# Attention over sixteen-wide heads: queries and keys turned unstacked and spread by transfers, row maxima turned alone

## The chip, the cores and the metric

One core of one Trainium2 chip runs the whole program. The metric is the device time of one execution in microseconds (us); less is better. A profiled execution also has a span, from its first to its last recorded instruction.

## What is computed

The program is a chain of six blocks over x, 4 batches of 512 tokens of width 256: a mixture of experts, attention, experts again, a gated feed-forward block, an attention on sine features, and the feed-forward block again. The change lies in the softmax attention alone:

```
q, k, v = split(x @ Wqkv + bqkv)          # 16 heads of 16
q, k = rot(q), rot(k)                     # rotary: t1*c - t2*s, t1*s + t2*c
scores = q @ k.T / 4 + causal_mask
ctx = softmax(scores) @ v
x = x + ctx @ Wout + bout
```

## The kernel before

All values are 32 bits wide. A value that TensorE multiplies in its one-pass format (F32R) is split in a high half (the value rounded to the format) and a low half (the rest), and products are summed over the halves. For a head, the 16 rows of the turned query stand three times on the partitions (high, low, high) and those of the key as high, high, low, so that one matmul over 48 partitions gives all three products. A 49th row holds the negated row maximum beside the queries and 1 beside the keys: the second product of a head then comes out with the maximum already subtracted. Two heads, a pair, stand at partitions 0 and 64.

Attention goes over 32 pairs `w` (4 batches of 8 pairs), with 3 steps `t` each, 96 steps in all and some more to drain. Step t of every engine's program holds, in this order written out by hand:

- TensorE (PE): `scores(t)` (L1343), query blocks against keys, to banks 0 and 1; `shifted(t - 7)` (L1358), the transposed product with the maxima, to banks 2 and 3; every sixth step and the one after it `weigh` (L1373), probabilities times v; then a turn, a set of four 128-column transposes to bank 4 (L1313): `turn_q1(s+1)` in the first step of a pair, `turn_k(s+1)` in the second, `turn_q2(s-1)` in the third, the last one with the maxima in the stack. Behind that the next batch's work (`turn_x`, `project_qk`, `project_v`; u is the step within the batch) and the last batch's (`turn_sums`, `turn_context`, `project_half`).
- VectorE (DVE): the copy of a turned key stack (`out_k`, L1730) in the third step, rotary pieces (`rope_a` L1716, `rotate` L1723), then `maxima(t)` (L1740), which frees the score banks for the next step.
- ScalarE (ACT): the copies of the two query turns (`out_q1` L1590, `out_q2` L1596), the copies of projections, `high` (L1583, L1584), which writes the high halves of the stacks, and `exponentials` (L1606).
- GpSimd (POOL): `keep_causal` (L1245), `swapped` (L1225), a rotary piece, and `low` (L1236), which writes the low halves.
- SyncE (SP): its queue has only loads ahead of the loop and stores of finished rows late in it.

Ahead of the loop (the lead) batch 0 is projected, its rotary pieces run on DVE alone, and the first pair is turned. `spin` (L337) is matmul work with no result, to keep PE busy.

Of the kernel before, what the change touches and what calls it, by code (L numbers as in the profile page):

```python
# [14 lines left out]
P = 128  # L15
# [207 lines left out]
def program(nc, ins, out):  # L223
# [4 lines left out]
    with ExitStack() as ctx:  # L228
# [33 lines left out]
        g.route_dram = nc.dram_tensor("route_rows", (2 * TILES, P), F32, kind="Internal").ap()  # L262
        g.xn_dram = nc.dram_tensor("xn_rows", (TOKENS, D), F32, kind="Internal").ap()
# [830 lines left out]
def attention_stage(nc, g, ins):  # L1094
# [3 lines left out]
    with ExitStack() as ctx:  # L1098
# [10 lines left out]
        rot = turns("rot", [P, 2, 2 * D])  # L1109
# [10 lines left out]
        part_b = sb("part_b", [P, 2, 2 * D])  # L1120
# [3 lines left out]
        q1 = sb("q1", [P, 2, SEQ], F32R)  # L1124
        q2 = sb("q2", [P, 2, SEQ], F32R)
        kt = sb("kt", [P, 4, SEQ], F32R)
# [8 lines left out]
        a_done, b_done, rot_done, hi_done, lo_done = (  # L1135
            sem("a_done"), sem("b_done"), sem("rot_done"), sem("hi_done"), sem("lo_done"))
        q1_ps, q1_out, k_ps, k_out, q2_ps, q2_out = (
            sem("q1_ps"), sem("q1_out"), sem("k_ps"), sem("k_out"), sem("q2_ps"), sem("q2_out"))
# [20 lines left out]
        bank_of = lambda m: AFTER[m][0]  # L1159

# [6 lines left out]
        def _(sp):  # L1167
# [9 lines left out]
            for b in range(2, BATCH):  # L1177
                sp.wait_ge(g.back_here[b - 2], 32)
                load_back(sp, g, b)
            def store_x(b):  # L1180
                sp.wait_ge(x_added, 2 * b + 2)
                sp.dma_start(by_tiles(g.turned_dram[0], b), g.x[:, b * BT:(b + 1) * BT, :]).then_inc(x_stored, 16)
# [4 lines left out]
            store_x(0)  # L1187
            store_x(1)
            store_xn(0)
            store_xn(1)  # L1190
# [11 lines left out]
        def _(pool):  # L1202
            nc.gpsimd.memset(b_src[:, :], 0.0).then_inc(zeroed, 1)
            for q in range(2):
                nc.gpsimd.memset(f32(k_stack[:, q, :, :, 3 * HD:SK]), 1.0)
                nc.gpsimd.memset(f32(q_stack[:, q, :, :, 3 * HD:SK]), 0.0)
                last = nc.gpsimd.memset(v[:, q, :, :, HD:HD + 1], 1.0)
            last.then_inc(ready, 1)
            norm.rstd(pool, 0)
# [8 lines left out]
            def swapped(n):  # L1218
                pool.wait_ge(qk_out, n + 1)
                if n >= 2:  # L1220
                    pool.wait_ge(rot_done, n - 1)
                src = qk[:, n % 2, :].rearrange("p (h s e) -> p h s e", s=2, e=HALF)
                dst = part_b[:, n % 2, :].rearrange("p (h s e) -> p h s e", s=2, e=HALF)
# [6 lines left out]

            def low(n):
                pool.wait_ge(hi_done, n + 1)
                b, i = n // BT, n % BT
                halves = rot[:, n % 2, :].rearrange("p (s h d) -> p s h d", s=2, d=HD)
                for s, (stack, hi, lo) in enumerate(((q_stack, 0, 1), (k_stack, 0, 2))):
                    last = nc.gpsimd.tensor_tensor(stack[:, b % 2, i, :, lo * HD:(lo + 1) * HD], halves[:, s, :, :],  # L1236
                                                   f32(stack[:, b % 2, i, :, hi * HD:(hi + 1) * HD]), ALU.subtract)
                last.then_inc(lo_done, 1)
# [10 lines left out]
            for i in range(BT):  # L1249
                low(i)  # L1250
            biased(0)
            norm.rstd(pool, 1)
            for t in range(ALL + LAG + 1):
# [4 lines left out]
                if front < BATCH:  # L1258
# [4 lines left out]
                    elif u == 8:  # L1263
                        low(4 * front)
                    elif u == 9:
                        low(4 * front + 1)
# [4 lines left out]
                    elif u == 13:  # L1271
                        low(4 * front + 2)
                    elif u == 14:
                        low(4 * front + 3)
# [9 lines left out]
        def _(pe):  # L1284
# [24 lines left out]
            def turn_stack(w, stack, bank, done):  # L1309
                b, hp = w // PAIR, w % PAIR  # L1310
                for i in range(BT):
                    flat = f32(stack[:, b % 2, i, :, :]).rearrange("p h c -> p (h c)")
                    last = nc.tensor.transpose(g.ps[:, bank, i * P:(i + 1) * P], flat[:, hp * P:(hp + 1) * P],  # L1313
                                               g.ident[:, :])
                last.then_inc(done, 1)

            def turn_q1(w):
                pe.wait_ge(lo_done, 4 * (w // PAIR) + 4)
                if w >= 3:
                    pe.wait_ge(q2_out, w - 2)  # L1320
                turn_stack(w, q_stack, 4, q1_ps)

            def turn_k(w):
                pe.wait_ge(q1_out, w + 1)
                turn_stack(w, k_stack, 4, k_ps)

            def turn_q2(w):
                pe.wait_ge(max_done, 2 * STEPS * (w + 1))
                pe.wait_ge(k_out, min(w + 3, BATCH * PAIR))
                turn_stack(w, q_stack, 4, q2_ps)  # L1330

            def scores(t):
                w, step = t // STEPS, t % STEPS
                if step == 0:
                    pe.wait_ge(q1_out, w + 1)
                    pe.wait_ge(k_out, w + 1)
                for a in range(2):
# [3 lines left out]
                    for i in SCORES[step]:  # L1341
                        n = (i + 1) * P
                        last = nc.tensor.matmul(g.ps[:, a, col:col + n], q1[at, w % 2, i * P:n], kt[at, w % 4, 0:n],  # L1343
# [4 lines left out]
            def shifted(t):  # L1348
                w, step = t // STEPS, t % STEPS
                if step == 0:  # L1350
                    pe.wait_ge(q2_out, w + 1)
                for a in range(2):
# [3 lines left out]
                    for j in SHIFTED[step]:  # L1356
                        n = SEQ - j * P
                        last = nc.tensor.matmul(g.ps[:, 2 + a, col:col + n], kt[at, w % 4, j * P:(j + 1) * P],  # L1358
                                                q2[at, w % 2, j * P:SEQ], start=True, stop=True)
# [61 lines left out]
            for i in range(BT):  # L1421
                if i >= 2:
                    pe.wait_ge(qk_out, i - 1)
                    pe.wait_ge(v_out, i - 1)
                project_qk(0, i, 2 + i % 2)
                project_v(0, i, 5 + i % 2)
            for i in (2, 3):
                pe.wait_ge(lo_done, i)
                spin(nc, g, 0, 10)
            turn_q1(0)  # L1430
            turn_k(0)
            for t in range(ALL + LAG + 5):
# [120 lines left out]
        def _(act):  # L1553
# [6 lines left out]
            def out_qk(b, i, bank):  # L1560
                n = 4 * b + i
                act.wait_ge(qk_ps, n + 1)
                if n >= 2:
                    act.wait_ge(a_done, n - 1)
                    act.wait_ge(b_done, n - 1)
# [9 lines left out]
            def high(b, i):  # L1575
                n = 4 * b + i
                act.wait_ge(rot_done, n + 1)
                if b >= 2:
                    act.wait_ge(q2_ps, PAIR * (b - 1))
                halves = rot[:, n % 2, :].rearrange("p (s h d) -> p s h d", s=2, d=HD)  # L1580
                cols = lambda stack: stack[:, b % 2, i, :, :].rearrange("p h (c d) -> p h c d", d=HD)
                twice = lambda s: halves[:, s, :, :].unsqueeze(2).to_broadcast([P, H, 2, HD])
# [1070 lines left out]
```

## Time and profile before

| | |
|---|---|
| median of 3 runs | 1167.85 us (1167.42 to 1170.57) |
| the profiled execution's own time | 1165.93 us |
| its span | 1164.0 us |
| PE busy over the span | 1052.2 us (90%) |
| DVE, ACT, POOL busy | 731.1, 463.2, 432.6 us |
| attention's loop (about 236.6 to 506 us) | some 270 us |

### The profile page before, as it was taken

The page shows a single profiled execution, that of the slowest core. Times are in us where ns is not written, and L with a number is a line of the kernel's source. Part 1 is how long each engine was busy: PE and PEld are TensorE (multiplying, and loading weights), DVE is VectorE, ACT ScalarE, POOL GpSimd, SP SyncE. Part 2 cuts the span into 40 slices and gives each one's busy share as a digit, 9 for nine tenths or more (in the row PEclk, how much of TensorE's full clock was granted, in tenths as well). Part 3 has the DMA queues.
Part 4 walks back from the last instruction along what each step waited for, and adds up shares of the span by engine and source line. Part 5 has one row for each costly group of instructions (what it writes and reads, how often), then busy time and mean ns, then how long its engine had stood idle before and what let it go on. Part 6 is the DMA issues. An engine that isn't in the chain of part 4 may idle for free. (4 is left out here: it accounts for less than half of the span.)

```text
span 1164.0 us, 18769 instructions
## 1 busy us (share of the span) xinstructions
PE 1052.2 (90%) x6537; PEld 870.1 (75%) x6537; DVE 731.1 (63%) x1754; ACT 463.2 (40%) x806; POOL 432.6 (37%) x474
## 2 busy tenths in 40 slices
PE   4899995779999999987999987999988998899997
PEld 3778884656566665666888886888878897788886
DVE  7934443787777778557454446765648878555653
ACT  4324331327666756625243322233334434223222
POOL 3056654326362723201576521000139788300000
PEclk8699998889989998887999998999997999999999
DMA  9034422300000000117472241000010030000000
GB/s 335 31 94 144 156 80 90 108 0 2 2 1 20 1 19 19 37 37 290 143 252 91 83 162 61 1 1 1 1 73 1 4 70 1 1 1 19 19 19 19
DMA packets 36881, 72.39 MB, mean 62 GB/s; under 512 B 8180, under 2 KB 25654, under 8 KB 36536
## 3 DMA queue, kind: packets, MB, share of 16 engines
q1 hardware_dynamic: 29112, 50.21, 12.8%
q0 software_dynamic: 7680, 20.98, 5.5%
q8 instruction: 57, 0.93, 0.3%
q14 instruction: 32, 0.26, 0.1%
HBM read 47.04 MB, written 24.13 MB: 61 GB/s over the span
## 5 line engine op out<-in xcount | busy, mean ns | idle before, releaser
L2041 PE MATMUL ps<-xt,w 128*128 128x512 f32 x768 | 192.5, 401 | 7.0 <-PEq L66 7.0
L2041 PEld LDWEIGHTS ps<-xt,w 128*128 128x128 f32 x768 | 143.3, 192 | 36.9 <-issue 5.5
L1740 DVE CUSTOM_DVE_ANT_0 ps<-ps,att_mask 128x128 f32<-128x128 f32 (+3 forms) x256 | 119.1, 516 | 40.6 <-PE ps L1343 40.3
L718 PE MATMUL ps<-moe_w,moe_narrow_xb 128*128 x480 | 125.0, 395 | 0.0
L122 POOL TENSOR_TENSOR var_eps<-bn,eps 128x4 f32<-128x4 f32 x24 | 6.6, 275 | 290.5 <-DVE bn L99 265.5
L2137 DVE TENSOR_TENSOR had_gated<-ps,had_sig 128x512 f32<-128x512 f32 x64 | 44.3, 691 | 110.8 <-ACT had_sig L2094 110.8
L2094 ACT ACTIVATE had_sig<-ps 128x512 f32<-128x512 f32 x64 | 38.3, 598 | 188.7 <-PE ps L2041 188.7
L616 POOL DMA_INDIRECT moe_xs<-xn_rows,moe_index x80 | 80.7, 1009 | 75.5 <-DVE moe_index L1017 44.1
L622 POOL DMA_INDIRECT made_rows<-moe_units_made,moe_index x80 | 79.6, 994 | 74.6 <-ACT moe_units_made L845 62.1
L718 PEld LDWEIGHTS ps<-moe_w,moe_narrow_xb 128*128 128x128 f32 x480 | 90.1, 188 | 19.6
L1606 ACT ACTIVATE att_early_probs<-ps 128x384 f32<-128x384 f32 (+1 forms) x192 | 90.7, 527 | 29.4 <-PE ps L1358 28.5
L1245 POOL TENSOR_SCALAR_AFFINE_SELECT att_early_probs<-att_early_probs 128x256 f32<-128x256 f32 x128 | 53.5, 431 | 118.1 <-ACT att_early_probs L1606 118.0
L1036 DVE TENSOR_TENSOR moe_narrow_xb<-ps,moe_narrow_xb 128x512 fp32r<-128x512 f32 x40 | 27.6, 691 | 110.2 <-ACT moe_narrow_xb L827 110.1
L2055 PE MATMUL ps<-w,had_yhi 128*128 128x256 f32 x512 | 94.4, 283 | 1.8 <-DVE had_ylo L2149 1.8
L2055 PEld LDWEIGHTS ps<-w,had_yhi 128*128 128x128 f32 x512 | 82.9, 189 | 7.8 <-DVE had_ylo L2149 2.6
L827 ACT ACTIVATE moe_narrow_xb<-ps 128x512 fp32r<-128x512 f32 x40 | 23.8, 598 | 135.0 <-PE ps L702 135.0
L1343 PE MATMUL ps<-att_kt,att_q 48*128 48x256 f32 (+3 forms) x256 | 66.4, 417 | 11.8 <-DVE att_q_stack L1740 9.1
L2055 PE MATMUL ps<-w,had_ylo 128*128 128x256 f32 x256 | 72.2, 282 | 0.0
L2277 POOL TENSOR_TENSOR fea_inv_norm<-fea_norm,neg_half 128x24 f32<-128x24 f32 x16 | 66.7, 4172 | 11.3 <-DVE fea_norm L2506 11.1
L337 PE MATMUL ps<-column,ident 128*128 128x128 f32 x356 | 53.5, 320 | 18.3 <-PEq L66 11.1
L744 PE MATMUL ps<-moe_w,moe_units_yb 128*128 x480 | 67.6, 280 | 0.0
L337 PEld LDWEIGHTS ps<-column,ident 128*128 128x128 f32 x356 | 51.7, 234 | 19.8 <-issue 11.2
(276 smaller groups left out, 2320.0 us busy)
## 6 DMA issues: line engine op xcount, KB each, us to landing
moe_w<-in_moe SPq DMA_DIRECT2D x16, 768.0 KB, 8.9
back<-made_rows SPq DMA_DIRECT2D x16, 512.0 KB, 5.7
x<-x_turned SPq DMA_DIRECT2D x8, 512.0 KB, 7.9
low_weights<-moe_w SPq DMA_DIRECT2D x4, 768.0 KB, 3.6
moe_w<-low_weights SPq DMA_DIRECT2D x4, 768.0 KB, 16.7
x<-in_x SPq DMA_DIRECT2D x4, 512.0 KB, 5.5
xn_rows<-moe_wide_xn SPq DMA_DIRECT2D x4, 512.0 KB, 10.7
x_turned<-x SPq DMA_DIRECT2D x4, 512.0 KB, 2.9
```

The costliest lines, as they stand in the source:

```text
L337: nc.tensor.matmul(g.ps[:, bank, 0:P], g.ident[:, :], g.column[:, :], start=True, stop=True)
L616: nc.gpsimd.indirect_dma_start(out=xs[:, j % AHEAD, i, :], out_offset=None, in_=g.xn_dram[:, :], in_offset=at(0, 2 * j + i)).then_inc(gath ...
L622: nc.gpsimd.indirect_dma_start(out=g.made_dram[:, :], out_offset=at(1, 2 * j + i), in_=made[:, j % 2, i, :], in_offset=None) \
L718: last = nc.tensor.matmul(h_bank(j, i), xb[a][:, j % 2, i, k, :], weight(c), start=False, stop=(k == KC - 1 and c == 1))
L744: last = nc.tensor.matmul(O_BANK[:, i * D:(i + 1) * D], yb[a][:, j % 2, i, c, :], weight(q), start=False, stop=(c == IC - 1 and q == 1), s ...
L1245: last = nc.gpsimd.affine_select(block, block, [[0, 2], [1, P]], ALU.is_ge, 0.0, base=0, channel_multiplier=-1)
L1343: last = nc.tensor.matmul(g.ps[:, a, col:col + n], q1[at, w % 2, i * P:n], kt[at, w % 4, 0:n], start=True, stop=True)
L1606: nc.scalar.activation(probs[:, w % 3, a, at:at + n], g.ps[:, 2 + a, 0:n], ACT.Exp, scale=HD ** -0.5).then_inc(exp_done, 1)
L1740: last = nc.vector.tensor_tensor_reduce(g.ps[:, a, col:col + n], g.ps[:, a, col:col + n], mask[:, SEQ - n:SEQ], -1.0, 3.0e38, ALU.add, ALU ...
L2041: last = nc.tensor.matmul(g.ps[:, bank(n, half), :], w[a][:, k, c * P:(c + 1) * P], xt[low][:, b % 2, k, :], start=(k == 0 and q == 0), st ...
L2055: last = nc.tensor.matmul(o, a[:, n % 4, at], g.w2[w][:, c, :], start=(c == 0 and q == 0 and i % 2 == 0), stop=(c == HC - 1 and q == 2), s ...
L2277: nc.gpsimd.tensor_tensor(inv_norm[:, t % 4, :], norm2[:, t % 4, :], g.neg_half[:, 0:QKH], ALU.pow) \
```

## The change

Queries and keys are no longer stacked before they are turned. Four chunks per batch (queries or keys of eight heads, 128 columns; `turn_chunk`) are turned as whole values; ACT writes the high half (`high_chunk`) and DVE the low half (`low_chunk`) of the chunk behind the turn, into `stage`. SP stores both halves to DRAM (`store_chunk`, 2 transfers of 256 KB) and loads them back onto their partitions (`load_chunk`, 6 transfers of 128 KB). The first pair's rows are copied directly, 6 transfers on SP and 6 on ACT. The maxima are written to `shift`, two columns for each block of rows, turned alone (`turn_shift`, 2 rows of 512), copied by ACT (`out_shift`) and put in the 49th row by two transfers of 2 KB (`place_shift`). The turns of the maxima stand in the second step of a pair and those of chunks in the third. In the lead the rotary piece `swapped` goes from DVE to POOL, and `rope_a` now waits for it; the stores of finished rows take their turn behind the loop's transfers.

```diff
-        q_stack = sb("q_stack", [P, 2, BT, H, SK], F32R)
-        k_stack = sb("k_stack", [P, 2, BT, H, SK], F32R)
-        kt = sb("kt", [P, 4, SEQ], F32R)
+        stage = sb("stage", [P, 2, 2, SEQ], F32R)
+        shift = sb("shift", [P, 3, BT, 2], F32R)
+        shift_row = sb("shift_row", [P, SEQ], F32R)
+        qt = sb("qt", [P, 2, H // 2, SEQ], F32R)
+        kt = sb("kt", [P, 2, H // 2, SEQ], F32R)
...
+        COPIES = ((0, 1, 0), (0, 0, 1))
+        def chunk_at(s):
+            if s in (1, 2):
+                return s + 1
+            b, c = (s // PAIR, 3) if s % PAIR == 0 else (s // PAIR + 1, s % PAIR - 5)
+            return 4 * b + c if s >= 5 and c >= 0 and b < BATCH else None
...
+            def store_chunk(n):
+                sp.wait_ge(chunk_hi, n + 1)
+                sp.wait_ge(chunk_lo, n + 1)
...
+                for half in range(2):
+                    sp.dma_start(g.spread_dram[c, half], f32(stage[:, n % 2, half, :])).then_inc(stage_stored[n % 2], 16)
+            def load_chunk(n):
...
+                sp.wait_ge(stage_stored[n % 2], 32 * (n // 2 + 1))
...
+                for a, rows, half in copies(n):
+                    mine = g.spread_dram[c, half].rearrange("(m a d) n -> a d m n", a=2, d=HD)[a]
+                    sp.dma_start(f32(stacked[n % 2][rows, b % 2, 4 * (c // 2) + begin:4 * (c // 2) + 4, :]),
+                                 mine[:, begin:, :]).then_inc(rows_here[c], 16)
+            def place_shift(w):
+                sp.wait_ge(shift_out, w + 1)
+                for a in range(2):
+                    at = 64 * a + 3 * HD
+                    sp.dma_start(f32(qt[at:at + 1, b % 2, hp, :]), f32(shift_row[a:a + 1, :])).then_inc(shift_here, 16)
...
+            for s in range(1, BATCH * PAIR + 1):
+                if chunk_at(s) is not None:
+                    store_chunk(chunk_at(s))
+                place_shift(s - 1)
+                if chunk_at(s) is not None:
+                    load_chunk(chunk_at(s))
...
+            def turn_rows(n, i):
+                return nc.tensor.transpose(g.ps[:, chunk_bank(n), i * P:(i + 1) * P], rot[:, i, at:at + P], g.ident[:, :])
...
+            def turn_shift(w):
+                pe.wait_ge(max_done, 2 * STEPS * (w + 1))
...
+                for i in range(BT):
+                    last = nc.tensor.transpose(g.ps[0:2, CHUNK_BANK, i * P:(i + 1) * P], f32(shift[:, w % 3, i, :]),
                                                g.ident[:, :])
...
-                if step == 0 and s + 1 < BATCH * PAIR:
-                    turn_q1(s + 1)
-                elif step == 1 and s + 1 < BATCH * PAIR:
-                    turn_k(s + 1)
-                elif step == 2 and 1 <= s <= BATCH * PAIR:
-                    turn_q2(s - 1)
+                if step == 1 and 1 <= s <= BATCH * PAIR:
+                    turn_shift(s - 1)
+                elif step == 2 and chunk_at(s + 1) is not None:
+                    turn_chunk(chunk_at(s + 1), s)
...
-                if step == 0 and 2 <= s < BATCH * PAIR + 2:
-                    out_q2(s - 2)
-                elif step == 1 and s + 1 < BATCH * PAIR:
-                    out_q1(s + 1)
+                if step == 2 and 1 <= s <= BATCH * PAIR:
+                    out_shift(s - 1)
+                elif step == 0 and chunk_at(s) is not None:
+                    high_chunk(chunk_at(s))
...
-                if step == 2 and s + 1 < BATCH * PAIR:
-                    out_k(s + 1)
+                if step == 0 and chunk_at(s) is not None:
+                    low_chunk(chunk_at(s))
```

## Rows read from the trace of the kernel before

**Rows 1.** Windows of the lead and of each batch's 24 steps.

```profile
core 0: us, PE busy (x) PEld busy (x) DVE busy (x) ACT busy (x) POOL busy (x), PEclk, DMA share, GB/s
211.00:236.60 25.60, 19.94 (x104) 17.48 (x104) 20.99 (x39) 8.91 (x17) 11.05 (x11) 0.83 0.09 30
236.60:300.00 63.40, 57.03 (x349) 37.63 (x350) 50.28 (x178) 36.77 (x74) 25.89 (x43) 0.89 0.00 1
300.00:363.00 63.00, 60.73 (x452) 41.00 (x452) 47.77 (x162) 40.70 (x85) 29.33 (x49) 0.95 0.01 1
363.00:428.00 65.00, 63.03 (x470) 42.56 (x467) 46.61 (x160) 42.65 (x89) 28.89 (x49) 0.95 0.03 9
428.00:484.00 56.00, 53.27 (x383) 32.31 (x383) 44.28 (x171) 33.76 (x69) 15.10 (x36) 0.88 0.09 30
```

**Rows 2.** Waits in the loop, 236 to 506: us in total, times, longest.

```profile
PEld ps L1343 <- DVE att_q_stack L1740: 14.8, 47, 0.8
PEld ps L1313 <- ACT att_q L1590: 5.2, 13, 0.5
```

**Rows 3.** Timeline of PE: start, length, instructions; a turn and what follows it.

```profile
371.48 0.66 PE L1313 MATMUL ps<-ident,att_q_stack 128*128 128x128 f32 x4
371.89 0.48 PE L1294 MATMUL ps<-att_b_row,ones 128*128 128x512 f32 x1
...
432.35 0.66 PE L1313 MATMUL ps<-ident,att_q_stack 128*128 128x128 f32 x4
432.93 0.50 PE L1343 MATMUL ps<-att_kt,att_q 48*128 48x128 f32 x4
```

**Rows 4.** Timeline of DVE: the third and the first step of two pairs, back to back.

```profile
295.64 0.68 DVE L1730 CAST att_kt<-ps 128x512 fp32r<-128x512 f32 x1
296.24 0.69 DVE L1740 CUSTOM_DVE_ANT_0 ps<-ps,att_mask 128x512 f32<-128x512 f32 x1
...
297.63 0.30 DVE L1740 CUSTOM_DVE_ANT_0 ps<-ps,att_mask 128x128 f32<-128x128 f32 x1
...
298.86 0.14 DVE L1740 DVE_READ_ACCUMULATOR2_ANT att_q_stack<- 128x1 fp32r x1
```

**Rows 5.** Groups by form, attention's whole stage.

```profile
L1225 POOL TENSOR_TENSOR att_part_b<-att_qk,att_rope_s 128x256 f32<-128x256 f32 x24 | 20.5, 875 | 16.0 <-ACT att_qk L1566 16.0
L1596 ACT ACTIVATE att_q<-ps 128x512 fp32r<-128x512 f32 x32 | 19.4, 607 | 8.2 <-PE ps L1313 8.1
L1206 POOL MEMSET att_q_stack<- 128x1024 f32 x2 | 1.9, 959 | 0.0
```

**Rows 6.** DMA issues with the median time to landing, then SP's timeline of issues.

```profile
x<-x_turned SPq DMA_DIRECT2D x8, 512.0 KB, 7.9
x_turned<-x SPq DMA_DIRECT2D x4, 512.0 KB, 2.9
route<-route_rows SPq DMA_DIRECT2D x1, 16.0 KB, 1.9
...
485.21 0.36 SPq L1182 DMA_DIRECT2D x_turned<-x  x1
578.52 2.00 SPq L575 DMA_DIRECT2D x<-x_turned  x4
```

**Rows 7.** Timeline of the end of the lead, all engines.

```profile
228.07 1.16 DVE L1723 TENSOR_TENSOR att_turns_rot<-att_turns_rot,att_part_b 128x512 f32<-128x512 f32 x1
230.95 4.31 DVE L1804 SCALAR_TENSOR_TENSOR x<-back,route,x 128x256 f32<-128x256 f32 x4
236.65 0.50 PE L1343 MATMUL ps<-att_kt,att_q 48*128 48x128 f32 x4 [0.88 <-DVE att_kt L1730]
237.70 0.29 DVE L1740 CUSTOM_DVE_ANT_0 ps<-ps,att_mask 128x128 f32<-128x128 f32 x1
```

**Rows 8.** Windows of 3.3 us in the loop, columns as in the first group.

```profile
325.70:329.00 3.30, 2.45 (x16) 1.49 (x14) 3.30 (x11) 2.61 (x6) 3.30 (x6) 1.00 0.00 0
329.00:332.30 3.30, 3.30 (x17) 3.15 (x17) 2.68 (x10) 1.47 (x3) 2.93 (x5) 0.51 0.00 0
...
464.30:467.60 3.30, 2.38 (x15) 1.62 (x14) 3.27 (x12) 0.71 (x2) 0.48 (x1) 1.00 0.44 153
470.90:474.20 3.30, 3.30 (x18) 2.17 (x20) 2.17 (x6) 1.68 (x3) 0.41 (x1) 0.50 0.03 7
```

More of the change, by code:

```diff
@@ L1159, in attention_stage, with chunks_turned, chunk_bank, copies @@
         bank_of = lambda m: AFTER[m][0]
+        COPIES = ((0, 1, 0), (0, 0, 1))
+        CHUNK_BANK = 4
+        LEAD_CHUNKS = 2
+        stacked = (qt, kt)
+        def chunk_at(s):
[3 more added lines that the diff above has]
+            return 4 * b + c if s >= 5 and c >= 0 and b < BATCH else None
+        def chunks_turned(s):
+            return LEAD_CHUNKS + sum(chunk_at(q) is not None for q in range(1, s + 1))
+        def chunk_bank(n):
+            return 0 if n == 1 else CHUNK_BANK
+        def copies(n):
+            for a in range(2):
+                for c, half in enumerate(COPIES[n % 2]):
+                    yield a, slice(64 * a + HD * c, 64 * a + HD * (c + 1)), half
         def at_step(t, offset):
@@ L1186, in store_xn @@
                 sp.dma_start(by_tiles(g.xn_dram[:, :], b), g.xn[:, b % 2, :, :]).then_inc(xn_stored[b], 16)
[L1187 to L1190, printed above, removed]
+            sp.wait_ge(chunk_hi, 1)
+            sp.wait_ge(chunk_lo, 1)
+            for a, rows, half in copies(0):
+                sp.dma_start(f32(qt[rows, 0, 0, :]), f32(stage[HD * a:HD * (a + 1), 0, half, :])).then_inc(direct_here[0], 16)
+            for n in range(LEAD_CHUNKS):
+                store_chunk(n)
+            for n in range(LEAD_CHUNKS):
+                load_chunk(n)
+            BESIDE = {2 * PAIR: (store_x, 0), 3 * PAIR: (store_x, 1), 3 * PAIR + 3: (store_xn, 0), 3 * PAIR + 6: (store_xn, 1)}
+            for s in range(1, BATCH * PAIR + 1):
[4 more added lines that the diff above has]
+                    load_chunk(chunk_at(s))
+                if s in BESIDE:
+                    store, b = BESIDE[s]
+                    store(b)
             store_x(2)
@@ L1229, in swapped @@
                 last.then_inc(b_done, 1)
[L1231 to L1238, printed above, removed]
             def keep_causal(t):
@@ L1249, in _ @@
             for i in range(BT):
-                low(i)
+                swapped(i)
+            set_ones(1)
             biased(0)
@@ L1332, in scores @@
             def scores(t):
                 w, step = t // STEPS, t % STEPS
-                if step == 0:
-                    pe.wait_ge(q1_out, w + 1)
-                    pe.wait_ge(k_out, w + 1)
+                b, hp = w // PAIR, w % PAIR
+                if w == 0 and step == 0:
+                    pe.wait_ge(chunk_hi, LEAD_CHUNKS)
+                    pe.wait_ge(chunk_lo, LEAD_CHUNKS)
+                    for kind in range(2):
+                        pe.wait_ge(direct_here[kind], 96)
+                elif step == 0:
+                    for kind in range(2):
+                        pe.wait_ge(rows_here[2 * (hp // 4) + kind], 96 * (b + 1))
@@ L1632, in _ @@
             act.wait_ge(ready, 1)
-            out_qk(0, 0, 2)
-            out_v(0, 0, 5)
-            for i in range(1, BT):
+            for i in range(BT):
                 out_qk(0, i, 2 + i % 2)
+            for i in range(BT):
                 out_v(0, i, 5 + i % 2)
-                high(0, i - 1)
-            high(0, BT - 1)
-            out_q1(0)
+            for n in range(LEAD_CHUNKS):
+                high_chunk(n)
+            act.wait_ge(chunk_hi, 2)
+            act.wait_ge(chunk_lo, 2)
+            act.wait_ge(ones_set, 1)
+            for a, rows, half in copies(1):
+                nc.scalar.dma_start(f32(kt[rows, 0, 0, :]), f32(stage[HD * a:HD * (a + 1), 1, half, :])) \
+                    .then_inc(direct_here[1], 16)
             for t in range(ALL + LAG + 5):
@@ L1836, in _ @@
                 rope_a(i)
-                swapped(i)
                 rotate(i)
-                if i == 1:
-                    add_back(2, 0)
+            for n in range(LEAD_CHUNKS):
+                low_chunk(n)
+            add_back(2, 0)
             dve.wait_ge(combined, 8)
@@ L1843, in _ @@
             add_back(2, 1)
-            out_k(0)
             for t in range(ALL + LAG + 5):
```

194 lines of the change are left out of this document (84 added, 110 removed).

## The prediction

> **What bounds the kernel now.** I read the page first: TensorE is busy for 90% of the span, so work taken from it can pay. The change touches one stage, so I cut that stage into its lead and its four batches with the windows view [rows 1]. In the second and third batch PE is busy for 60.73 of 63.0 us and 63.03 of 65.0, DVE for 47.77 and 46.61: PE's own instructions set the pace there. In the last batch PE has 53.27 of 56.0 and DVE 44.28, in the first 57.03 of 63.4 and 50.28. The waits view says what ends PE's few pauses: the maxima, which free the score banks, with 14.8 us of late weight loads in 47 places, and the query copy with 5.2 us in 13 [rows 2]. So PE binds, and DVE's maxima stand close behind it in steps where PE has little else to do. The reader is to see that second bound before subtracting anything.
>
> **PE: turns removed and added.** Before, 96 sets of four transposes are turned (32 each of q1, k and q2). After, there are 16 chunk sets and 32 shift sets. Two sets leave the lead (the first pair's q1 and k) and two come into it (chunks 0 and 1), so the loop goes from 94 to 46 sets: 48 fewer. By batch it is 10, 12, 12 and 14 fewer (before 23, 24, 24 and 22, after 13, 12, 12 and 8, and behind the last step one in each). A set keeps PE 0.41 us when projection work follows (371.48 to 371.89) and 0.58 us ahead of scores (432.35 to 432.93) [rows 3]. I take 0.5 us: 24 us in all, or 5, 6, 6 and 7 us by batch. A shift set moves the same 128 columns of the identity four times; no row shows one with two stationary columns. Its bounds are nothing and 0.58 us, and I charge it as a full set, the nearest row; were it free, another 32 x 0.5 = 16 us would lie with PE.
>
> **What DVE lets through.** DVE needs 1.39 us for the third step's maxima (296.24 to 297.63) and 1.37 us for the first step's (297.63 to 299.00); the key copy ahead of them takes 0.60 us (295.64 to 296.24) [rows 4]. The second step's, two instructions of 384 columns, I estimate at 1.1 us, between. A pair thus can't go under 3.9 us, a step under 1.3 us on the mean. Where a step holds only scores, shifted and a turn, PE needs about 1.3 us now, and taking 0.5 us off it gives nearly nothing; where a step has a projection, `weigh` or a context turn behind it (some 9 of 12 places in a middle batch) all of it counts. DVE loses 32 key copies and gains 14 low halves in the loop, 18 x 0.60 = 11 us less, which helps just in those short steps. I keep 5 of 6 us in each middle batch, 6 of 7 in the last, and 3 of 5 in the first, whose early steps wait for DVE's added rows. Sum: 19 us.
>
> **The clock takes some back.** When PE has pauses its granted clock falls: the slice from 325.7 us has PE busy for 2.45 of 3.3 us while DVE is full, and the next slice runs at 0.51, which is the 1.2 GHz level; the same at 464.3 us with 2.38, and 0.50 soon after [rows 8]. By batch the clock is 0.89, 0.95, 0.95 and 0.88 [rows 1]; one minus the clock, times the window, is 7.0, 3.2, 3.3 and 6.7 us of PE time lost, 20 us. Fewer turns make more such pauses. One more dip is a slice of 3.3 us at half speed, 1.65 us of PE work. I charge one more in each of the first three batches (5 us) and 2 us in the last, where the dips fall on steps that DVE bounds: 7 us. The Trainium skill, "TensorE: Matmul & The Clock Gate", section "A second HAM failure mode: psum-queue depth-cycling", says that micro-idles between groups of matmuls make the clock oscillate and lower throughput even where single matmuls look fast. The trace agrees with the direction; by that rule alone the gain might vanish, by my row it is cut by a third. Loop: 19 - 7 = 12 us.
>
> **The lead.** Before, the last rotary piece ends at 229.23 us, scores start at 236.65 and the first maximum at 237.70; between them DVE has a row addition of 4.31 us [rows 7]. After, swapped runs on POOL at 2 x 0.875 us a tile against DVE's 1.5, and four tiles alternate between two buffers; projections of v come after those of q and k. I work out the last rotary piece at 224 to 226, PE's last chunk turn at 226, its copy at 226.7, both low halves at 228. Six direct transfers at 0.4 to 0.5 us of issue and 1.9 us to landing [rows 6] give 232.5. But DVE still owes two row additions, statistics and a normalisation (8 us) before the first maximum: 236, some 1.5 us early. Bounds: 4 us early if the additions run uncontended, 4 us late if the direct copies land at 240. The ones for `kt`, 4096 columns, cost POOL 4 x 0.959 = 3.8 us [rows 5], as much as the four stack memsets that go. Then the second pair: 4 stores (1.5 us of issue), landing in 2.9 us each, then 12 loads at 0.5 us, 6 us, and 2 to 3 us to land. That is about 241.5 against a need at about 243 (step 3, 7 to 8 us behind the start). I charge 1 us for late rows, here and of the maxima. With the 1.5 gained: 0.5 us.
>
> **The path of the maxima.** Before, PE, ACT and PE again; now PE turns, ACT copies 2 x 512 (0.607 us for 512 columns [rows 5]), SP issues two transfers, and `shifted` waits for both. From the turn's end: about 0.9 us until the copy is done, behind the exponentials, two issues of 0.36 us, and 1.9 us of landing by the smallest transfer that has one [rows 6]: 3.4 us. The cover is the rest of that step, two steps and the next scores. With projections or `weigh` this is 4 to 8 us; in bare steps, which I put at 1.4 us after the change, it is 3.1 us. By the order of the steps some 3 pairs of 32 have 3.1 us, 2 have 4, 7 have 4.8 and 20 more than 5.5. Only the first 3 are late, by 0.3 us each: the 1 us charged above. Transfers of one row from SBUF to SBUF are not in the trace; landing lies between nothing and the 7.9 us of a 512 KB load. At 4 us and more most pairs are late. The Trainium skill, "DMA: Bandwidth & Descriptors", section "Rules for kernel authors", says that many small transfers should be coalesced, since below 64 KB one pays mostly overhead. That speaks against 64 transfers of 2 KB; it changes the time only if the overhead shows on PE, which is the second rival.
>
> **SP's queue.** In a pair with a chunk SP has 2 stores, 2 rows and 6 loads: 2 x 0.36 + 2 x 0.36 + 6 x 0.5 = 4.4 us of issue in a pair of some 6.5 us. What waits behind the loads is the next store and then the next row, 5 us later; it fits. A chunk's rows are loaded at least 3 steps ahead of their use, 7 us or more against 6 loads (3 us) and 3 to 5 us to land. ACT loses 64 copies and 24 `high` instructions in the loop and gains 46 copies: no bound before, less after. The finished rows' stores wait for SP by a step or two; nobody needs them before the next stage.
>
> **Sum.** 1165.93 - 12 - 0.5 = 1153.4 us for a profiled execution; the median lies 1.92 us above that before, so 1155.
>
> **The rivals.**
> - *The clock takes the whole gain.* For: batches with the least spare work already run at 0.88. Every second slice of the last batch and three more dips in each other would cost 3.3 + 15 us. Against: a slower PE fills its own pauses, and the 0.95 batches are packed with projections. Time: 1165 to 1169. Chance 0.14.
> - *The rows with the maxima land late: slower.* If one lands 5 us after issue instead of 1.9, the path is 6.5 us, and the pairs above wait 3 x 3.4 + 2 x 2.5 + 7 x 1.7 + 20 x 0.5 = 37 us: 1155 + 37 = 1192 us. It turns the sign where landing exceeds some 3.6 us, where the first three terms are 6 + 2 + 3 = 11 us and PE's new pauses bring a dip or two. Against: an otherwise empty DMA (share 0.00 to 0.09 in rows 1). Chance 0.14.
> - *DVE is not in the way and shift sets are cheap.* Nearly all 24 us come, and a third of the 16 us in the shift sets, with no more dips: 1138 to 1145. Chance 0.12.
> - The forecast case, 6 to 20 us faster: 0.60.
>
> **How the numbers follow.** A measurement of this kernel can tell 0.3%, 3.5 us, from no change. Faster: 0.60 + 0.12 and a little of the first rival, 0.73. Same: 0.13. Slower: 0.14. The likeliest case alone reaches from 1148 to 1162. For 8 in 10 the range takes in the first rival and the nearer half of the third: 1143 to 1169.
>
> **What the profile would show.** Turn sets fall from 96 to 48 with 0.4 to 0.6 us each; batches 2 and 3 of 58 to 61 us; a clock of 0.85 to 0.93 in the loop; waits of scores on the maxima grown from 15 us to 20 or 30. The wait of `shifted` for the row's transfer should total under 5 us, and that of `scores` for loaded rows show once, at the second pair. The prediction is wrong if the first of these waits is tens of us, if scores start later than 240 us, or if the clock falls below 0.85.

## The result and the profile after

The changed kernel is slower, by 1.0%. In paired runs on one chip it took 1183.56 us (median of 4, 1180.16 to 1186.44) and the kernel before 1169.21 (median of 4, 1167.42 to 1173.14): ratio 1.0104, 95% interval 1.0064 to 1.0144. The forecast was 1155 us.

| | before | after |
|---|---|---|
| profiled execution's own time / span | 1165.93 / 1164.0 us | 1180.16 / 1178.3 us |
| PE busy | 1052.2 us | 1049.6 us |
| DVE, ACT, POOL busy | 731.1, 463.2, 432.6 us | 718.7, 435.9, 415.0 us |
| mean granted clock | 0.935 | 0.909 |

Every engine is less busy, and the time is longer. The windows view of the changed kernel, cut at the first scores of each batch and at the last scores (columns as in [rows 1]):

```profile
233.10:299.90 66.80, 54.73 (x289) 32.87 (x289) 48.05 (x168) 28.73 (x58) 18.88 (x33) 0.74 0.57 116
299.90:371.20 71.30, 64.11 (x417) 39.04 (x416) 47.44 (x168) 37.00 (x79) 23.90 (x44) 0.83 0.38 76
371.20:434.80 63.60, 57.88 (x417) 36.52 (x416) 44.91 (x155) 36.08 (x76) 22.26 (x41) 0.92 0.45 93
434.80:488.80 54.00, 50.21 (x321) 25.15 (x320) 39.17 (x160) 28.21 (x60) 14.61 (x35) 0.75 0.32 68
```

Against [rows 1] PE issues 35 to 62 instructions fewer in a batch, yet its busy time in the second has risen, and the granted clock is down in all four, by the most in the first, second and last. Waits of the changed kernel, 225 to 520 us (total, times, longest):

```profile
PE ps L1403 <- DVE att_shift L1790: 21.1, 34, 2.2
PE ps L1403 <- DMA att_kt<-spread_rows: 3.9, 1, 3.9
...
PE ps L1403 <- DMA att_kt<-att_stage: 2.2, 1, 2.2
```

The same view for the weight loads:

```profile
PEld ps L1403 <- DVE att_shift L1790: 30.0, 65, 1.4
```

L1403 is now the line of `scores`, L1420 that of `shifted`, L1382 that of `turn_shift`, L1790 that of the maxima. Weight loads wait for the maxima 30.0 us where they waited 14.8 [rows 2], and the scores' matmuls 21.1 us. Late transfers show twice: ahead of the first scores, 2.2 us, and ahead of the second pair's, 3.9 us. `shifted` waits for the transfer of the maxima in one place only, 0.5 us ahead of a weight load.

To say where time goes I cut each trace's loop (first to last scores) by one rule. *Pauses* are stretches in which no matmul runs. *Clock loss* is half of the remaining time that the trace grants at 1.2 GHz. *Work* is what is left. The three add up to the loop; they are worked out from the start and length of every matmul and from the granted clock, and each trace's batches in us stand beside them:

```
                 batch 1  2     3     4     loop   work   pauses  clock loss  at 1.2 GHz
before           60.5   65.3  64.8  54.5   245.1  211.8   13.3    19.9        41.0
changed          66.7   71.4  63.6  54.0   255.7  183.3   28.7    43.6        95.6
```

The first two batches lose 6.2 and 6.1 us, the last two gain 1.2 and 0.5. The turns' removal came: work is 28.5 us less. Pauses took back 15.4 and the clock 23.7: the loop is 10.6 us longer. Behind the loop, attention's last work took 38.9 us instead of 35.7. The scores start 3.5 us earlier (233.14 against 236.65), and attention's end is 10.3 us later. The last 4 us of the 14.3 between the two spans stand behind attention, where the program is the same; on another chip that part of the two kernels did not differ (668.1 us before, 668.4 changed, first experiment), so I don't put them down to the change.

How one fall of the clock looks, in three windows of 3.3 us of the changed kernel:

```profile
315.50:318.80 3.30, 2.45 (x16) 1.35 (x14) 2.12 (x8) 2.13 (x6) 2.21 (x4) 1.00 0.02 4
318.80:322.10 3.30, 2.78 (x10) 1.61 (x10) 3.30 (x13) 1.91 (x5) 3.11 (x6) 0.52 0.02 5
322.10:325.40 3.30, 3.30 (x9) 2.16 (x10) 1.12 (x5) 0.90 (x2) 0.39 (x1) 0.50 0.01 1
```

PE has pauses in two windows (2.45 and 2.78 busy of 3.30) and runs at half speed from the second on. The third has nine matmuls, all of it busy: this is step 7 of the second batch, a projection, which takes 5.60 us at 1.2 GHz, and 3.39 us in the third batch at full speed. Its 2.2 us are lost on work that nothing covers.

### The profile page after: what moved, and what is told of

It is laid out like the page before. It is cut to its first block and busy times, and to the rows that moved or that the text cites. A ratio compares the mean times of both kernels' runs of the same rounds, so it can differ in the third digit from the quotient of the medians.

```text
span 1178.3 us, 18490 instructions
## 1 busy us (share of the span) xinstructions
PE 1049.6 (89%) x6347; PEld 851.7 (72%) x6347; DVE 718.7 (61%) x1730; ACT 435.9 (37%) x758; POOL 415.0 (35%) x448
## 5 line engine op out<-in xcount | busy, mean ns | idle before, releaser
L1790 DVE CUSTOM_DVE_ANT_0 ps<-ps,att_mask 128x128 f32<-128x128 f32 (+3 forms) x256 | 119.1, 515 | 47.7 <-PE ps L1403 47.3
L623 POOL DMA_INDIRECT made_rows<-moe_units_made,moe_index x80 | 79.4, 993 | 78.5 <-ACT moe_units_made L846 66.4
L1403 PE MATMUL ps<-att_kt,att_qt 48*128 48x256 f32 (+3 forms) x256 | 73.0, 453 | 28.6 <-DVE att_shift L1790 21.1
L1403 PEld LDWEIGHTS ps<-att_kt,att_qt 48*128 48x128 f32 x256 | 35.8, 211 | 68.0 <-issue 36.4
L828 ACT ACTIVATE moe_narrow_xb<-ps 128x512 fp32r<-128x512 f32 x40 | 23.7, 596 | 135.0 <-PE ps L703 135.0
## 6 DMA issues: line engine op xcount, KB each, us to landing
moe_w<-low_weights SPq DMA_DIRECT2D x4, 768.0 KB, 16.4
```

The lines of the kernel that those rows point to most:

```text
L623: nc.gpsimd.indirect_dma_start(out=g.made_dram[:, :], out_offset=at(1, 2 * j + i), in_=made[:, j % 2, i, :], in_offset=None) \
L1403: last = nc.tensor.matmul(g.ps[:, a, col:col + n], qt[at, b % 2, hp, i * P:n], kt[at, b % 2, hp, 0:n], start=True, stop=True)
L1790: last = nc.vector.tensor_tensor_reduce(g.ps[:, a, col:col + n], g.ps[:, a, col:col + n], mask[:, SEQ - n:SEQ], -1.0, 3.0e38, ALU.add, ALU ...
```

## The experiments

The loop table of all experiments, by the same rule (the first two are the kernels before and changed, run again on a second chip):

```
                 batch 1  2     3     4     loop   work   pauses  clock loss  at 1.2 GHz
e8_before        62.3   66.4  64.8  54.5   248.0  209.9   12.4    25.7        54.6
e7_changed       66.7   71.5  63.6  54.1   255.9  183.4   29.0    43.6        95.6
e1_shift3        71.4   73.5  70.8  59.2   274.9  209.8   27.5    37.6        81.4
e2_before_less   60.6   64.7  67.7  56.1   249.0  186.9   16.4    45.8        95.6
e3_more_stores   69.4   68.3  66.5  57.6   261.8  181.3   32.1    48.4       109.0
e4_spins         70.8   66.3  65.8  51.8   254.7  193.7   25.2    35.8        75.1
e5_refill        66.1   68.2  67.8  56.0   258.1  228.8   16.0    13.3        30.7
e6_fill0         68.0   66.4  66.8  55.4   256.7  212.3   24.0    20.4        47.8
e9_aimed         68.0   65.0  61.8  55.2   250.1  200.9   22.7    26.5        58.0
e10_before_aimed 62.3   62.5  63.7  50.4   238.9  220.7    9.8     8.3        17.1
```

They ran on three other chips, on which the kernel before takes 1194.6 to 1196.6 us; ratios are to it on the same chip. Each row of the table is one profiled execution, and what lies outside the loop took 944 to 961 us in them, so ratios of whole times and loops need not agree to the microsecond.

**The two kernels again (e7_changed, e8_before).** No edit.

> The changed kernel as it is, on the chip and in the hour of its neighbours here. Both theories: 1.0 to 1.4% over the kernel before. Half-clock time in the loop 80 to 105 us.

> The kernel before as it is, for its profile beside the others. Clock theory: half-clock time in the loop of 35 to 55 us here too, against 80 to 105 us in the changed kernel. If it is over 70 us, the clock doesn't tell the two kernels apart.

1217.54 us, ratio 1.0137 (1.0058 to 1.0216), and 1201.33, ratio 1.0025 (0.9987 to 1.0062). The changed kernel's loop is 255.9 us with the same 95.6 us at 1.2 GHz as on the first chip, batch by batch within 0.1 us, both inside what was expected. In batches 2 and 3 the clock falls in the same steps in both executions, so these falls are no accident of one execution; in the last batch some stand a few steps apart. The kernel before has nine falls on both chips, but they are longer here: 54.6 us at 1.2 GHz against 41.0, the upper end of what was expected. One of 3.3 us stands in step 7 of its second batch, where the first chip has none, though the pauses ahead are the same. Its loop is 248.0 us against 245.1, its clock loss 25.7 against 19.9: of two executions of one kernel, 3 us in the loop and 6 us in the clock are the scatter of such a table.

**More work in the turns of the maxima (e1_shift3).** Each shift set does its four transposes three times.

```diff
-                for i in range(BT):
+                for i in 3 * list(range(BT)):
```

> Changed kernel, with each set of shift turns done three times: 64 sets of four transposes more in the loop, as many matmul instructions as the kernel before has and some 25 us of PE work at 0.4 us a set. Clock theory (the lost turns had kept PE's clock up): half-clock time in the loop falls from about 95 us to 50 to 70 us and the time stays or falls, 1168 to 1184 us. Work theory (PE's own work is what is paid for): 1200 to 1210 us. Theory of late transfers: the sets lie in steps before the rows are needed, so nothing changes there; by itself it gives 1184 to 1190 us, with no change in the clock.

1227.83 us, ratio 1.0263 (1.0176 to 1.035); the loop is 19 us longer. Work rose by 26.4 us for 64 sets, 0.41 us a set; pauses fell by only 1.5 and clock loss by 6. A shift set with two stationary columns is therefore not free, as I had left open, and work in the second step of a pair, where PE had paused little, is for the most part paid. This is what the work theory had expected: the ratio makes some 1200 us of the first chip's 1169.21, its range was 1200 to 1210, and the clock theory's 50 to 70 us at half clock came out at 81.4. Making up the number of instructions does not bring the clock back. The added work is transposes, that of e5 and e6 is matmuls; no run put one in the other's place, so place and kind are not told apart here.

**Less work in the kernel before (e2_before_less).** `turn_q1` and `turn_k` transpose one block instead of four, and ACT and DVE copy that block four times; three quarters of the query's first turn and of the key's are left out, 192 of 384 transposes, or 48 sets, 46.5 of them in the loop, where the change removes 48. Nothing else of the change is in it. One transpose of each such set stays in its place, which the change doesn't leave.

```diff
-                for i in range(BT):
+                for i in range(BT if done is q2_ps else 1):
...
-                nc.vector.tensor_copy(kt[:, w % 4, :], g.ps[:, 4, :]).then_inc(k_out, 1)
+                nc.vector.tensor_copy(kt[:, w % 4, :].rearrange("p (i n) -> p i n", n=P),
+                                      g.ps[:, 4, 0:P].unsqueeze(1).to_broadcast([P, BT, P])).then_inc(k_out, 1)
```

> Kernel before, with only one of the four transposes in each turn of q1 and of k; its 128 columns are copied four times over, so queries and keys of the later blocks are those of the first. 192 transposes fewer, as many as the change takes from the loop, and no transfer, no chunk, no move of any other work. Clock theory: half-clock time in the loop grows from 41 us to 70 to 100 us and eats most of the 20 to 24 us of work: 1158 to 1176 us. Theory that the change loses by its transfers, waits and moves: the clock stays and the time is 1145 to 1151 us.

1204.79 us, ratio 1.0066 (1.002 to 1.0112): taking the work out alone, with no transfer, makes the kernel no faster, and by the ratio slightly slower. The theory of transfers and moves had 1145 to 1151 us on the first chip's scale and the clock as it was; the clock theory's 70 to 100 us at half clock came, 95.6, and its 1158 to 1176 us was just passed (some 1177). Its windows, by batch:

```profile
251.40:311.90 60.50, 53.32 (x280) 32.84 (x280) 48.49 (x169) 34.18 (x69) 24.78 (x41) 0.77 0.00 1
311.90:376.60 64.70, 61.74 (x417) 38.41 (x416) 49.30 (x171) 43.21 (x90) 30.42 (x52) 0.87 0.00 1
376.60:444.30 67.70, 64.50 (x417) 40.55 (x416) 46.82 (x158) 42.67 (x88) 28.87 (x49) 0.82 0.03 9
444.30:500.40 56.10, 53.07 (x331) 29.65 (x331) 42.87 (x166) 32.41 (x66) 14.69 (x35) 0.76 0.09 29
```

The instruction counts are those of the changed kernel (417 in the middle batches) with a DMA share near nothing, and the clock has fallen to 0.77, 0.87, 0.82 and 0.76. Against e8: 23.0 us less work, 4.0 more in pauses, 20.1 more in the clock. This run alone decides against the forecast: the removed work is worth nothing here, with no help from the transfers. Its profiled execution is the fastest of its ten (1195.01 us), e8's the slowest of its eight (1207.74); the difference lies outside the loop. Between e8 and e7 pauses grow by 16.6 us and clock loss by 17.9; 4.0 us of pauses and a clock loss as large (20.1) come with the removed work by itself, so 12.6 us of pauses are the change's own, and they add nothing to the clock loss. By the step, 7.8 of these 12.6 us stand in the first steps of pairs, where the change leaves no turn and e2 one transpose, 4.3 in the third and 0.6 in the second. Clock loss therefore doesn't follow the sum of the pauses: e2 and e7 both have 95.6 us at 1.2 GHz, with pauses of 16.4 and 29.0.

**More stores (e3_more_stores).** From the fifth chunk on, both halves are stored a second time to memory that nobody reads: 2 transfers of 256 KB more for each of 12 chunks. The chunk's loads wait for all four stores, by a further line of the edit, and so start later too.

```diff
+                if n >= 4:
+                    for half in range(2):
+                        sp.dma_start(g.unused_dram[n, half], f32(stage[:, n % 2, half, :])).then_inc(stage_stored[n % 2], 16)
```

> Changed kernel, with the stores of chunks 4 to 15 done twice, the second time to DRAM that nobody reads; the loads wait for both. 12 x 512 KB more DMA and later loads. Transfer theory (contention or late rows cost time): 5 to 15 us slower than the changed kernel. Clock theory: within 0.3% of it, since no row of the loop is waited for after the second pair.

1219.76 us, ratio 1.0196 (1.0124 to 1.0267); the loop is 5.9 us longer than e7's. In this trace `shifted` does wait for the transfer of the maxima, 5.4 us in three places, where e7's waits once, 1.0 us. So the path of the maxima has cover for the change's own transfers, and little to spare: it was my second rival, and doubling the stores with later loads is enough to begin it. The 5.9 us are at the low end of the transfer theory's 5 to 15. Pauses make 3.1 of them and the clock 4.8, with 2.1 less in work; the clock's part is no larger than the scatter above. On the medians, 1219.76 against e7's 1217.54 on another chip, the two can't be told apart.

**Longer spins at the start (e4_spins).** The idle time ahead of the first scores and at the wait for the second pair's rows is filled with spin.

```diff
-            spin(nc, g, 1, 8)
+            spin(nc, g, 1, 40)
...
+                if t == 3:
+                    pe.wait_ge(xlo_done, 4)
+                    spin(nc, g, 5, 40)
```

> Changed kernel, with 32 more empty matmuls ahead of the first scores and 40 ahead of the second pair's, to cover the waits of 2.2 and 3.9 us for transferred rows with work. Clock theory: of some 34 us at half clock in the first batch 10 to 15 go, 3 to 7 us faster than the changed kernel. Theory of late rows: the waits end when they ended, within 0.3% of it or up to 2 us slower by the spins that overrun.

1217.08 us, ratio 1.0155 (1.0063 to 1.0247). The spins outlast the waits, and the first batch grows to 70.8 us; the others lose less to the clock. The loop comes out at 254.7 us against 255.9, and the 3 to 7 us that the clock theory had expected did not come. The edit was too coarse to decide anything.

**Filling the first step of every pair and the third where no chunk is turned (e5_refill), or the first alone (e6_fill0).** A set of four matmuls of `ident` by `column`, 128 columns each and to a bank that nobody reads, stands where turns stood before: 49 sets in e5, 31 in e6.

```diff
+            def fill(s, step):
+                if step == 0:
+                    pe.wait_ge(chunk_lo, chunks_turned(s))
+                for i in range(BT):
+                    nc.tensor.matmul(g.ps[32:64, CHUNK_BANK, i * P:(i + 1) * P], g.ident[:, 0:32], g.column[:, :],
+                                      start=True, stop=True)
...
+                elif step == 2 and 1 <= s < BATCH * PAIR:
+                    fill(s, 2)
+                elif step == 0 and 1 <= s < BATCH * PAIR:
+                    fill(s, 0)
```

> Changed kernel, with a set of four empty 128-column matmuls in the first step of each pair and in the third where no chunk is turned: 49 sets, about as many as the change takes away, at the places in the step from which it takes them. No transfer, copy or wait for data differs but a wait for the chunk's low half. Clock theory: half-clock time in the loop falls from about 95 us to 40 to 55 us, and the loop is as long as the changed kernel's or up to 10 us shorter although PE has 24 us more work. Work theory: 15 to 24 us slower than the changed kernel, clock as it was.

> As the one before, with the sets of the first step of a pair alone (31 sets, 12 to 15 us of PE work). Clock theory: half-clock time in the loop of 60 to 80 us, a time within 5 us of the changed kernel. Work theory: 10 to 15 us slower.

e5: 1220.19 us, ratio 1.0165 (1.0079 to 1.0251). e6: 1211.96, ratio 1.0107 (1.0071 to 1.0143). Windows of e5 by batch:

```profile
247.90:314.00 66.10, 55.42 (x362) 35.52 (x362) 49.67 (x171) 29.47 (x60) 20.16 (x35) 0.90 0.59 117
314.00:382.20 68.20, 66.88 (x514) 45.16 (x514) 46.51 (x165) 35.64 (x76) 23.27 (x43) 0.95 0.42 80
382.20:450.00 67.80, 66.17 (x513) 44.96 (x512) 44.61 (x155) 36.01 (x76) 22.07 (x41) 0.95 0.44 88
450.00:506.00 56.00, 53.64 (x443) 34.40 (x442) 39.23 (x160) 27.42 (x60) 14.63 (x35) 0.97 0.32 67
```

With the transfers all there and useless work in place of the turns, the clock is back at 0.90 to 0.97. e5 adds 45.4 us of work, 0.93 us a set and well over the 24 that I had expected and the 28.5 that the change removed, and lengthens the loop by 2.2 us: 30.3 come back from the clock and 13.0 from pauses. e6 adds 28.9 for 0.8 us. Time at 1.2 GHz is 30.7 and 47.8 us, under even what the clock theory had expected (40 to 55, 60 to 80); the work theory had the clock as it was. In whole time e5, e6 and e7, all on one chip, are 1220.19, 1211.96 and 1217.54 us, near or inside e7's own range (1208.38 to 1223.00). This is e2's experiment from the other side, with more work put in than had been taken out. Matmuls wait for transfers 7.7 us in e5's trace and 6.5 in e7's: the fills didn't remove these waits.

**Filling the pauses alone (e9_aimed, e10_before_aimed).** I read each step's pause from the traces and put 1 to 4 such matmuls into the steps whose pauses come ahead of a fall: in the changed kernel at the end of up to four steps in each batch, in the kernel before ahead of the second query turn (the one with the maxima, in the third step) of ten pairs, 19 matmuls. Both also spin 12 times at the loop's fourth step, and e9 eight times more ahead of the first scores.

```diff
+            FILL = {2: 4, 5: 3, 6: 3, 11: 4}
+            FILL_LAST = {0: 4, 5: 2, 11: 2, 17: 4}
```

and in the kernel before

```diff
+            AIM = {2: 3, 8: 1, 10: 3, 12: 1, 16: 1, 18: 3, 20: 1, 24: 1, 26: 1, 28: 4}
...
+                spin(nc, g, 4, AIM.get(w, 0))
```

> Changed kernel, with 2 to 4 empty matmuls (0.21 us each) just where its trace shows PE pausing 0.4 to 1.1 us for the maxima: at the ends of steps 2, 5, 6 and 11 of a batch, of 0, 5, 11 and 17 of the last, and spins of 8 and 12 ahead of the two waits for rows. Some 12 us of PE work in pauses. Clock theory: half-clock time in the loop from 96 to 30 to 60 us, the loop from 256 to 235 to 245 us, at or under the kernel before. Work theory: the loop as long as before or longer by up to 12 us. Theory that transfers and their waits cost the time: the loop stays at 250 to 256 us.

> Kernel before, with 1 to 4 empty matmuls ahead of ten of its turns, where its own trace shows PE pausing for the maxima, and 12 ahead of the fourth step. Clock theory: half-clock time in the loop from 41 us (55 in another run) to 10 to 35, the loop 5 to 12 us shorter than 245 to 248 us. Work theory: the same time or 2 to 5 us longer.

e9: 1197.99 us, ratio 1.0045 (1.0016 to 1.0074). e10: 1189.57 us, ratio 0.9927 (0.9893 to 0.9962), faster than both kernels; the median of all its twelve executions is 0.4% under the kernel before. Windows of e10 by batch:

```profile
249.30:311.50 62.20, 57.49 (x358) 38.93 (x358) 48.02 (x169) 34.29 (x69) 24.76 (x40) 0.89 0.00 1
311.50:374.00 62.50, 61.17 (x474) 41.29 (x474) 49.01 (x171) 43.08 (x90) 30.42 (x52) 1.00 0.00 1
374.00:437.70 63.70, 62.77 (x475) 42.28 (x474) 46.28 (x158) 42.53 (x88) 28.87 (x49) 0.97 0.03 10
437.70:488.10 50.40, 47.58 (x385) 29.48 (x384) 42.63 (x166) 32.38 (x66) 14.59 (x35) 1.00 0.10 33
```

Five matmuls more in the second batch (each stands as two instructions in the counts) bring its clock from e8's 0.92 to 1.00 and its length from e8's 66.4 us (65.3 on the first chip) to 62.5; the last batch goes from 54.5 to 50.4. In the whole loop 10.8 us of work buy 17.4 us of clock and 2.6 of pauses. The loop's 238.9 us are 9.1 under e8's, as the clock theory had expected (5 to 12).

e9's middle batches take 65.0 and 61.8 us, against e7's 71.5 and 63.6 and e8's 66.4 and 64.8; but e10's take 62.5 and 63.7, so with both filled the changed kernel gains nothing in these two. Its loop of 250.1 us misses the 235 to 245 of the clock theory and lies where the theory of transfers and their waits had it, 250 to 256, although its time at 1.2 GHz fell from 95.6 to 58.0 us. The first batch is 68.0 us against e10's 62.3, with 10.4 us of pauses left in it, and the last one has a single stall of 4.0 us. The trace's answers on the tile with the maxima and on SP's issues there:

```profile
  PE ps L1432: 4.0, 1
...
DMA to landing us min/median/max: 1.6/1.7/5.7
```

```profile
454.71 0.43 SPq L1233 DMA_DIRECT2D x_turned<-x  x1
455.18 18.03 SPq L1229 DMA_DIRECT2D att_qt<-att_shift_row  x6
```

L1432 is `shifted` in e9. One row of maxima took 5.7 us to land instead of 1.7. The second line gathers the six issues of three pairs; the first stands 0.5 us behind a store of finished rows (512 KB), and behind a chunk's six loads. That the store delayed it is what the order suggests; no run moved the store.

## Why the prediction was wrong

**What bounds the kernel: right, and read too simply.** PE does set the pace. But the bound is PE at the clock that it is granted, and taking work out lowered that clock (e2) as putting work in raised it (e5, e6, e10), so its work and its speed can't be changed one at a time.

**PE's turns: right in kind, small by a sixth.** 48 sets fewer were charged with 0.5 us each, 24 us; 28.5 us of work went on the first chip and 26.5 between e8 and e7. In e2 23.0 went. A shift set costs somewhat less than the 0.5 that I charged, 0.35 us here where a projection follows (columns: start, length):

```profile
382.87 0.60 PE L1382 MATMUL ps<-ident,att_shift 128*2 128x128 f32 x4
383.22 0.47 PE L1345 MATMUL ps<-att_b_row,ones 128*128 128x512 f32 x1
```

and e1's extra sets 0.41 us, against a full set's 0.41 where a projection follows [rows 3]. The third rival, all 24 us and a third of the 16 in the shift sets, had the removed work about right at 29; what failed in it is "no more dips". Two of my counts were one too high, which changes nothing: 31 key copies leave the loop and 63 query copies.

**What DVE lets through: the mechanism right, the size a third.** I kept 19 of 24 us, 5 lost to pauses. Pauses grew by 15.4: 9.8 in the first steps of pairs, 4.5 in the third and 1.2 in the second. Matmuls of scores wait 21.1 us for the maxima where they waited 9.1. The late transfers are little of the growth: the first, 2.2 us, lies ahead of the loop, and the second, 3.9 us, stands where the kernel before paused nearly as long for the maxima:

```profile
244.63 1.35 PE L1343 MATMUL ps<-att_kt,att_q 48*128 48x128 f32 x4 [3.12 <-DVE att_q_stack L1740]
```

A pair of rows shows a pause in a short step. PE of the changed kernel, where no turn stands between the third step's and the next scores:

```profile
385.36 0.34 PE L1420 MATMUL ps<-att_qt,att_kt 49*128 49x384 f32 x2
386.46 0.88 PE L1403 MATMUL ps<-att_kt,att_qt 48*128 48x128 f32 x3 [0.77 <-DVE att_shift L1790]
```

Before, the same step was as long, 1.44 us, with a pause of 0.17: the turn had filled the other 0.6. I had expected no gain from such steps, rightly; I did not see that what is not gained there is a pause, with a price later.

**The clock: the step that failed.** I wrote "I charge one more in each of the first three batches (5 us) and 2 us in the last: 7 us". It was 23.7 us, which turns the loop's forecast of -12 into +4.7; the pauses' 15.4 instead of 5, with 4.5 us more of removed work, make the rest of the measured +10.6. I had priced one fall from a row, 1.65 us, rightly for its 3.3 us: half of a fall's length is what it costs. Their number and their length I had guessed. The loop has 14 falls instead of nine, and they last 6.8 us on the mean instead of 4.6; I had charged some four more of 3.3 us, and 54.6 us came. I had also argued that dips fall on steps that DVE bounds. Many don't: in the second batch a pause of 1.4 us in step 18 is followed by a step 20 of 4.87 us, all of it at half speed, instead of the 2.44 us of the kernel before. That removed work lowers the clock is shown by e2, that added work in these places raises it by e5, e6 and e10; that single pauses are what lowers it is how I read the traces, and no run shows it by itself. The rule that I had weighed beside the rows, the Trainium skill's "TensorE: Matmul & The Clock Gate", section "A second HAM failure mode: psum-queue depth-cycling", says that micro-idles make the clock oscillate; by that rule the whole gain could vanish, and the trace agrees, with the clock at 0.74, 0.83, 0.92 and 0.75 by batch.

**The rivals.** The first, that the clock takes the whole gain, is the mechanism; its 1165 to 1169 us supposed that the clock would stop at taking what was gained. In e2 the clock takes just about the gain, with a loop 1.0 us over e8's and a ratio of 1.0066. The rest of the loss goes with the 12.6 us of pauses that are the change's own. My argument against it, that packed batches are safe, failed in the second batch: 0.95 before, 0.83 after. The second rival (late rows of maxima, chance 0.14) forecast a slower kernel, which came, but not in this way: rows landed in 1.7 us in the middle (estimate 1.9), and `shifted` waited 1.0 us at most in the two traces of the changed kernel. It does begin in e3, with stores doubled.

**The lead and the queues.** Scores start 3.5 us earlier and the first maximum stands at 234.73 against 237.70. Some 1.8 us of that had been gained ahead of attention already (its first work starts at 205.40 instead of 207.19), so the lead gained about 1.2, near the forecast 1.5. Direct copies were put at 0.4 to 0.5 us of issue; six took 4.06 us on SP, 0.68 each. Loads of 128 KB land in 4.1 us at the median and not 2 to 3, and the 96 KB loads of the second pair's keys in 4.1 as well. PE waited 3.9 us for these rows; the maxima let the same scores start at 241.37 and they started at 244.23, so the rows were 2.9 us late and not 1:

```profile
spread_rows<-att_stage SPq DMA_DIRECT2D x32, 256.0 KB, 4.2
...
att_qt<-spread_rows SPq DMA_DIRECT2D x42, 128.0 KB, 4.1
...
att_qt<-att_shift_row SPq DMA_DIRECT2D x64, 2.0 KB, 1.7
```

**The signs that I had named.** The clock "below 0.85" was the one sign of being wrong that came true: over the four windows it is 0.81. The changed batches 2 and 3 were to take 58 to 61 us and took 71.3 and 63.6; scores' waits on the maxima reached the named 30.

**What stays open.** With fills in both, the changed kernel's first batch stays 5.7 us behind; its late rows are part of that, and no run moves the first loads alone. Why the change has 12.6 us of pauses more than e2 is not shown beyond the steps in which they stand. Why step 7 falls in the second batch and not in the third (5.60 and 3.39 us) stays open too: the nearest pause ahead, 0.61 us in step 6, is the same, those in steps 0 and 2 are 0.5 and 0.1 us longer in the second, and no run varied one pause at a time. In the kernel before the same step 7 fell in e8's second batch and neither in its third nor on the first chip, with the same pauses in steps 5, 6 and 7 (0.17, 0.09 and 0.2 us), and e10's third batch has that fall with the first two of them filled (0.00 and 0.04). So the pauses next to a fall do not foretell it.

## What to carry to other kernels

When TensorE is the bound and a second engine stands close behind it, cut each stage into work, pauses and time at the lower clock before pricing removed TensorE work. Ask of each removed instruction whether it filled a pause: here 48 sets worth 23 to 28 us came out at no gain by themselves, and at a loss with the rest of the change. Look first at the pauses that are already there, since 31 matmuls with no use, put in chosen steps, made the kernel before 0.7% faster with nothing else changed (0.4% by the medians of all executions).

## What the hardware showed that I had not expected

- 45 us of useless work cost the changed kernel 2.2 us of its loop.
- The falls of the clock repeat: two executions of the changed kernel on two chips each have 95.6 us of the loop at 1.2 GHz, though the chips differ by 27 us in the whole. Falls last 3.4 to 17.1 us in the first of them.
- In the two middle batches of the changed kernel a pause of 1.4 us in step 18, 4.06 us long, is followed by 6.8 and 3.4 us at half speed.
- A 2 KB row from SBUF to SBUF lands in 1.7 us at the median. Once, in e9, it took 5.7 us, with a 512 KB store and six 128 KB loads issued just ahead of it; that these held it up is not shown.
